# Sixteen copies of the relative node numbers in DRAM, one for each eight partitions of a spreading load

## The reference, cut to what matters

```python
x = x + gated_layer(relu(layernorm(x)))          # L0
h = relu(layernorm(x))                           # L1 begins
for i in range(2):
    xl = (h @ Wl[i] + bl[i]).reshape(n, 4, 128)
    xr = (h @ Wr[i] + br[i]).reshape(n, 4, 128)
    s = leaky_relu(xl[src] + xr[dst], 0.2)       # one row for each edge
    e = einsum('ehc,hc->eh', s, att[i])
    alpha = softmax of e over the edges of each dst
    out = segment_sum(alpha * xl[src], dst).mean(heads) + bias[i]
    h = relu(layernorm(out + h) * ln_g[i] + ln_b[i])
x = x + h                                        # then L2 (mean aggregate) and L3 (two SAGE layers)
```

## Time and profile before

| | |
|---|---|
| median of 3 runs | 3330.59 us |
| profiled execution | 3309.18 us |
| its span, first to last instruction | 3307.4 us |
| mean granted TensorE clock | 0.920 |
| VectorE busy | 2255.2 us (68%) |
| TensorE matmul busy | 2544.1 us (77%) |
| GpSimd busy | 817.6 us (25%) |
| two score phases | VectorE's L1059 from 674.6 to 1312.8 us, and to 2418.1 us in the second layer |

### The profile page before, as it was taken

How to read it: one execution, slowest core, us unless ns; L and a number is a source line. 1 busy time by engine, 2 the same in 40 slices (tenths; PEclk the granted TensorE clock), 3 DMA queues, 4 the chain that set the end, 5 groups by cost and what they waited for, 6 DMA issues and landing times. The chain is left out here.

```text
span 3307.4 us, 52083 instructions
## 1 busy us (share of the span) xinstructions
PE 2544.1 (77%) x12613; PEld 1548.7 (47%) x12613; DVE 2255.2 (68%) x10815; ACT 976.2 (30%) x2329; POOL 817.6 (25%) x856
## 2 busy tenths in 40 slices
PE   3775894878888887388867888888837884979898
PEld 2443783334444444266733444444425663434444
DVE  5667567868888888844686888888894446242223
ACT  2775891500000001133642000000012345333232
POOL 0000000056666665000003666666610000000000
PEclk8998997889999999699978999999968997989999
DMA  0000600389989896165425989998816542500100
GB/s 25 1 1 3 263 1 21 109 257 280 283 283 287 278 285 214 32 174 160 108 80 197 284 279 283 282 284 276 286 32 144 162 123 62 232 1 7 34 1 20
DMA packets 395806, 507.12 MB, mean 153 GB/s; under 512 B 29036, under 2 KB 331495, under 8 KB 394119
## 3 DMA queue, kind: packets, MB, share of 16 engines
q0 software_dynamic: 66560, 274.39, 25.1%
q1 hardware_dynamic: 327714, 227.61, 23.8%
q10 hardware_dynamic: 1252, 1.80, 0.2%
HBM read 409.08 MB, written 94.61 MB: 152 GB/s over the span
## 5 line engine op out<-in xcount | busy, mean ns | idle before, releaser
L939 POOL DMA_INDIRECT rows<-row_table,idx x832 | 793.2, 953 | 778.5 <-POOLq L134 307.0
L990 PE MATMUL z_ps<-xr,hot_ta 128*128 x2496 | 692.0, 387 | 207.5 <-DVE rows L1033 168.6
L1001 PE MATMUL z_ps<-rows,ident 128*128 128x256 f32 x1664 | 572.7, 426 | 5.0 <-issue 3.5
L990 PEld LDWEIGHTS z_ps<-xr,hot_ta 128*128 128x128 bf16 x2496 | 243.4, 98 | 511.5 <-issue 407.6
L2136 PE MATMUL dense_ps<-cnt,h 128*128 128x512 f32 (+1 forms) x1050 | 416.5, 555 | 85.2 <-ACT cnt L2094 81.5
L1033 DVE SCALAR_TENSOR_TENSOR rows<-rows,att_all 128x128 f32<-128x128 f32 x1664 | 421.6, 289 | 32.8 <-remote 19.2
L1059 DVE TENSOR_TENSOR rows<-z_ps,rows 128x256 f32<-128x256 f32 x832 | 347.8, 418 | 115.4 <-PE z_ps L1001 82.9
L1033 DVE SCALAR_TENSOR_TENSOR rows<-z_ps,att_all 128x128 f32<-128x128 f32 x1664 | 410.0, 281 | 13.0 <-issue 12.9
L1376 PE MATMUL acc_m<-xr,hot_m 128*128 x1984 | 341.9, 294 | 77.2 <-issue 52.1
L1376 PEld LDWEIGHTS acc_m<-xr,hot_m 128*128 128x128 f32 x1984 | 284.0, 195 | 141.6 <-issue 136.1
L2094 DVE CAST cnt<-counts 128x512 f32<-128x512 uint16 (+1 forms) x261 | 103.0, 397 | 329.9 <-PE dense_ps L2136 306.2
(11 more groups left out here) (399 smaller groups left out, 3148.6 us busy)
## 6 DMA issues: line engine op xcount, KB each, us to landing
xr<-kept_rows SPq DMA_DIRECT2D x124, 512.0 KB
kept_rows<-rows SPq DMA_DIRECT2D x416, 128.0 KB
spread_a<-rel_rows SPq DMA_DIRECT2D x208, 128.0 KB
counts_line<-counts SPq DMA_DIRECT2D x1, 19550.0 KB
counts<-counts_line SPq DMA_DIRECT2D x6, 3200.0 KB
rows<-row_table,idx POOLq DMA_INDIRECT x832
row_table<-xl_ring SPq DMA_DIRECT2D x50, 258.0 KB
rows<-row_table SPq DMA_DIRECT2D x32, 320.0 KB
```

Of the source, the lines that this page charges most:

```text
L939: nc.gpsimd.indirect_dma_start(out=rows[:, u, :], out_offset=None, in_=table, in_offset=bass.IndirectOffsetOnAxis(ap=c.idx[:, n:n + 1], ax ...
L990: nc.tensor.matmul(ps[:, n % Z, :], hot, tile[:, m, 0:HC], start=m == 0, stop=False, skip_group_check=True)
L1001: nc.tensor.matmul(ps[:, n % Z, HALF_C:HC], c.ident[:, :], rows[:, n % ROWS, HALF_C:HC], start=False, stop=True, skip_group_check=True).th ...
```

## The change

`rel_rows` becomes 16 copies, each SLOTS * 128 + 1024 elements long (54272 elements, 108544 bytes), so the copies begin 108544 bytes apart. In `make_slots` the two stores of `rel_rows` go. In their place SP issues four stores, one for each block of 104 slots, behind the loads of `dst_prev` and `dst_next`; each writes its block to all 16 copies, in pieces of 256 bytes. They count a semaphore of their own (`rel_out`), on which SP waits at the end of the phase. SP's earlier wait is now for three stores instead of five. In `gat_scores` partitions 0 to 7 of a spreading load read copy 0, partitions 8 to 15 copy 1, and so on. The 16 rows behind the end are gone.

```diff
+COPIES = 16
+COPY = SLOTS * P + 1024
...
                 sp.wait_ge(s["row_parts"], 2)
-                sp.dma_start(rel_rows[0:SLOTS * P].rearrange("(b r e) -> r b e", r=SB, e=P),
-                             rel_row[:, :, :]).then_inc(s["rows_out"], 16)
-                sp.dma_start(rel_rows[SLOTS * P:(SLOTS + WIDE) * P].rearrange("(r e) -> r e", e=P),
-                             rel_row[0:WIDE, 0, :]).then_inc(s["rows_out"], 16)
                 sp.dma_start(dst_line[1:1 + SLOTS * P].rearrange("(b r e) -> r b e", r=SB, e=P),
                              dst_row[:, :, :]).then_inc(s["rows_out"], 16)
                 for at in (0, 1 + SLOTS * P):
                     sp.dma_start(dst_line[at:at + 1].rearrange("(a e) -> a e", a=1),
                                  outside[:, :]).then_inc(s["rows_out"], 16)
-                sp.wait_ge(s["rows_out"], 5 * 16)
+                sp.wait_ge(s["rows_out"], 3 * 16)
                 for to, at in ((dst_prev, 0), (dst_next, 2)):
                     sp.dma_start(to[:, :, :], dst_line[at:at + SLOTS * P].rearrange("(b r e) -> r b e", r=SB, e=P))\
                       .then_inc(s["rows_back"], 16)
+                for b in range(SLOT_BLOCKS):
+                    sp.dma_start(bass.AP(rel_rows.tensor, b * SB * P, [[P, SB], [COPY, COPIES], [1, P]]),
+                                 rel_row[:, b, :].unsqueeze(1).to_broadcast([SB, COPIES, P]))\
+                      .then_inc(s["rel_out"], 16)
+                sp.wait_ge(s["rel_out"], SLOT_BLOCKS * 16)
...
                 def load(k):
-                    sp.dma_start(spread[:, k % HOTS, :], bass.AP(rel_rows.tensor, k * HALF * P,
-                                                                 [[0, P], [1, HALF * P]]))\
+                    sp.dma_start(spread[:, k % HOTS, :], bass.AP(rel_rows.tensor, k * HALF * P, [[COPY, COPIES], [0, P // COPIES],
+                                                                                      [1, HALF * P]]))\
                       .then_inc(s["spread"][k % HOTS], 16)
...
-    rel_rows = nc.dram_tensor("rel_rows", ((SLOTS + WIDE) * P,), BF16, kind="Internal").ap()
+    rel_rows = nc.dram_tensor("rel_rows", (COPIES * COPY,), BF16, kind="Internal").ap()
```

More of the change, by code:

```diff
@@ L211, in make_slots @@
                    before=0, m_before=0, picked=0, m_picked=0, slots=0, m_slots=0, rel=0, turned=0, broken=0, breaks=0,
-                   m_win=0, m_turned=0, row_parts=0, rows_out=0, rows_back=0) as (block, s):
+                   m_win=0, m_turned=0, row_parts=0, rows_out=0, rel_out=0, rows_back=0) as (block, s):
             whole = EDGES_FULL // P * P
```

## The result

| | median | range | runs |
|---|---|---|---|
| before | 3332.21 us | 3327.87 to 3336.59 | 7 |
| changed | 3342.90 us | 3335.97 to 3348.54 | 7 |

The ratio is 1.0037, with a 95% interval of 1.0027 to 1.0047: the change makes the kernel 0.37% slower, 10.7 us. Forecast was 3216 us, 115 us faster, with a range of 3172 to 3290.

What follows compares the result with a forecast made beforehand. Score phases were taken as bound by VectorE, with stops every four slots from spreading loads sharing one kilobyte. Relief 113 us plus phase starts 2 minus stores 0 gave 115 us, from 3330.6 to 3216 us, range 3172 to 3290.

Steps and rivals of the forecast that it cites:

- The step that failed: Score phases: VectorE and TensorE wait for a third; DMA throughput falls once in four slots and everything stands.
- the dips of the earlier trace: Score phases: DMA rate falls to 130 to 230 GB/s about 2 to 3 us behind a spreading load; should vanish.
- Is it the address?: Spreading loads: 128 partitions read one kilobyte, one DRAM place serves 16 DMA engines at 131 GB/s, and gathers stand behind.
- The gain, 113 us: Score phases: full relief wins back VectorE's idle time, 94 to 154 us, taken as 113; chance 0.70.
- The floor of VectorE: Score phases: VectorE's work of 1.334 us a slot, which the change doesn't touch, limits the gain.
- The loads "keep their issue on SP": Score phases: the spreading loads keep their number, size (128 KB) and issue on SP, with no cost set for it.
- The start of the phases, 2 us: Start of each score phase: VectorE's 8.7 us wait for the first loads shrinks by 2 us in all.
- The stores, 0 to 1 us: `make_slots`: four stores take 15.4 us at 111 GB/s, hidden behind VectorE's instructions; cost 0 to 1 us, taken as 0.
- B: Rival, score phases: a burst of 128 pieces in SP's queue makes the trough, not the address; no relief, 3330 us; chance 0.10.
- C: Rival, score phases: the 16 copies collide in one DRAM part and loads last longer, 77 us slower, 3408 us; chance 0.06.

Runs made afterwards that it cites:

- i2_no_loads: Kernel before with only the first three spreading loads of each score phase, on the 3311 us chip: 3310.11 us, ratio 0.9998 to the kernel before.
- g4: Kernel before with each spreading load issued three times, pattern in three dimensions, one shared address: 3366.53 us, against 3333.58 with two dimensions.
- h3: Kernel before with 10 row buffers instead of 14 and the load's pattern in three dimensions, one shared address: 3150.26 us, against 3141.08 with two dimensions.
- e4_stores_only: Changed kernel with the old load (all partitions read copy 0), on a 3116 us chip: 3115.69 us, ratio 1.0000 to the kernel before.
- e3_one_place_3dim: Kernel before with only the load's pattern changed to three dimensions, address still shared by all, on a 3116 us chip: 3115.43 us, ratio 0.9997.
- f1_after_again: The whole changed kernel once more, against the kernel before on a 3116 us chip: 3116.53 us, ratio 1.0004.
- e1_no_loads: Kernel before with only the first three spreading loads of each score phase, on a 3116 us chip: 3115.57 us, ratio 0.9999.

## Why the prediction was wrong, point by point

**The step that failed** is in the first part: "Two engines that wait for each other, with six banks between them, must be waiting for a third", and then that throughput falls "and everything stands". The third was taken to be the gathers, slowed by the spreading loads. i2_no_loads refutes it: without the loads the stops and the pace stay (0.9998). The evidence had been there. The earlier trace rows show VectorE's waits without a DMA, a stop between two instructions with no semaphore between them, and TensorE's idle time before the matmul that reads a gather, which was not brought into the argument, is 5.0 us in the whole kernel. Nor do the two engines wait for each other; they stand at the same time. What looked like proof, that the stops end about 3 us behind a spreading load, was rhythm: the median distance between VectorE's stops (over 0.25 us, neighbours joined) is 6.1 us, four slots, in the kernel before and also in i2_no_loads, where the load isn't there. And the dips of the earlier trace rows are no cause: in the changed kernel the DMAs move 275 GB/s in the stops and 277 overall.

**Is it the address?** The step that a shared kilobyte is slow was right, but shown with the wrong reach. It costs up to 213 us with three loads each and 27 us with ten row buffers. With 14 buffers and one load the slack of the phase hides it.

**The gain, 113 us.** Worked out from all of VectorE's idle time, as if one cause had made all of it. What the loads could give on this chip is nothing, by i2_no_loads. The floor of VectorE was right to 4%: 1.334 us a slot forecast, 1.289 us where VectorE is busy all the time.

**The loads "keep their issue on SP".** Wrong: 339 ns became 527 ns, with the third dimension. This is a likely part of the 10.7 us, since the form alone was slower wherever there was no slack (33 us in g4, 9 us in h3), and the copies alone were never slower where they could be told apart. But in those runs gathers were late, and on the chip with the stops they are not. Form and copies were not run apart there, so this is argued, not shown, and the gathers' longer packets stay a rival.

**The start of the phases, 2 us.** VectorE's wait went from 8.7 to 7.9 us: 0.8 us. The term was too large.

**The stores, 0 to 1 us.** Right: e4_stores_only is at 1.0000, and in the trace after SP's L700, the first issue of the next phase, starts at 575.62 us where it was 575.80. The cover held. The rate was better than taken. A window over most of the four stores, with the end of the loads before them (it moves 1.86 MB):

```profile
557.00:567.00 10.00, 0.00 (x0) 0.00 (x0) 9.00 (x29) 0.00 (x0) 0.00 (x0) 0.50 0.83 186
```

At 186 GB/s the 1.70 MB take 9.2 us, not 15.4. A price that the sum lacked is SP's own: issuing one such store takes it 2.18 us (median, 7.8 us for the four), where the old store took 0.34. The cover hid that too.

**The rivals.** B, that the trough isn't the address's and nothing comes of it, had 0.10 and is the nearest: its time, 3330, is 13 us off, and its mechanism (a burst in SP's queue) was wrong too, since the loads don't matter at all. C, copies that collide, was given 3408 us and did not happen: q1's packets took less time, not more (5.18 us of engine time a slot, before 5.81). What the Trainium skill's row on the step between copies says (DMA: Bandwidth & Descriptors, Latency and other measured facts) is not contradicted by it.

**What stays open.** What holds VectorE, TensorE and GpSimd at once for 0.9 us on average (65 stops of VectorE in the 500 us of i2_no_loads), mostly four slots apart, on some chips, 195 to 216 us of the kernel's time. The runs exclude the spreading loads, and TensorE's idle times exclude gathers that land late. Not left out on such a chip, and so not excluded, are GpSimd's issuing of the gathers and the load on the DMA engines that they make, the stores of `kept_rows`, and what else comes once in four slots: VectorE's one-hot (L1029) and the load of the slots' node tiles into TensorE's registers (L970, 82 times in 500 us). Why the change costs 0.4% on such a chip is open as above.

## What to carry to other kernels

Before a common stop of several engines is given to a transfer, find the instruction that reads the transfer's data and look whether its engine is idle before it, whatever releaser is named; compare when each engine stopped with when the count that it waits for was made, before one is called the follower of the other. A stop that ends between two instructions with no semaphore between them belongs to something else. A thing that comes in the same rhythm as the stop proves little when everything in the loop has that rhythm: leave it out and look, on a chip that shows the stop. A broadcast of one small piece to 128 partitions is dear for the DMA engines only when they are the limit, and then more different places are better, with the fewest dimensions in the pattern.

## What the runs showed of the hardware that was not expected

- The same program takes 3116 us on four chips (medians 3115.78 to 3116.59) and 3311 us on a fifth; the first comparison had 3332. The granted TensorE clock is the same (0.92), and in the score phase it is 0.98 to 1.00 on both kinds.
- The two kinds disagree on the worth of a change: ratio 1.0004 on one, 1.0037 and 1.0040 on the other, each beyond the other's interval.
- With three loads for one, reading 128 different places instead of one raises what the 16 DMA engines move, beside the same gathers, from 317 to 378 GB/s.
- One more dimension of step 0 in a load's pattern, for the same bytes, lengthens SP's issue from 339 to 521 ns (e3_one_place_3dim).
- Shorter packets in one queue can come back as longer packets in the other: q1 gave 0.63 us of engine time a slot and q0 took 1.37. On the chips of 3116 us (e4_stores_only against f1_after_again) it is 0.45 and 0.74.
- On the chips that have the stops, the profile itself is thinner in the score phases. The same kernel, e1_no_loads and i2_no_loads, left 10967 and 3403 recorded semaphore updates from 700 to 1200 us, and 2708 and 2707 up to 600 us. What loses the records, and whether it is what makes the stops, isn't shown.
